# A two-direction scan block: where the absolute step sizes are read from, and where the fusion products stand in TensorE's order

## What is computed

```python
xz = x @ Win.T;  u, z = split(xz, 2)
uc = silu(convb + sum_k shift(u, k) * convw[:, k])      # 4 taps along the sequence
x_dbl = uc @ Wx.T                                       # 16 columns for dt, 32 for B, 32 for C
dt = softplus(x_dbl[..., :16] @ Wdt.T + bdt)
h_t = exp(dt_t * A) * h_(t-1) + dt_t * u_t * B_t        # the scan along the sequence
y = (h . C + uc * Dp) * silu(z)
out = layernorm(y @ Wout.T)
```

## Time and profile before

| | |
|---|---|
| median of 3 runs | 4335.14 us (4325.14 to 4340.07) |
| the profiled execution | 4339.85 us |
| its span, first to last instruction | 4338.3 us |
| mean granted clock of PE | 0.905 |
| scan stage | about the first 2,500 us |
| busy over the span: PE / DVE / ACT / POOL | 92% / 84% / 66% / 54% |

### The profile page before, as it was taken

One profiled execution on the slowest core, in us unless ns is written; L12 is line 12 of the kernel. 1 busy time (PEld: TensorE's weight loads), 2 busy tenths in 40 slices (PEclk: granted clock), 3 DMA queues, 4 the chain that ended last, 5 costly groups with the idle time before them and its releaser, 6 DMA issues. The chain is left out here.

```text
span 4338.3 us, 69764 instructions
## 1 busy us (share of the span) xinstructions
PE 4001.3 (92%) x19212; PEld 2993.2 (69%) x19213; DVE 3654.2 (84%) x6958; ACT 2850.2 (66%) x4732; POOL 2333.2 (54%) x1949
## 2 busy tenths in 40 slices
PE   6999999999999999999999959999999699999998
PEld 4666566566666666665665647887888588888887
DVE  7999999999999999999999938887888666666665
ACT  5777777777777777777777746666666344454444
POOL 2454545445454544545454456666666545555555
PEclk8989989888998989899898879888888799999999
DMA  2122121222222222222222212222222255555555
GB/s 69 46 45 42 46 42 47 42 48 46 42 47 41 47 42 48 46 42 45 42 48 42 43 47 88 78 79 75 78 78 79 107 99 94 96 104 93 87 95 85
DMA packets 198461, 272.58 MB, mean 63 GB/s; under 512 B 23377, under 2 KB 143058, under 8 KB 198354
## 3 DMA queue, kind: packets, MB, share of 16 engines
q0 software_dynamic: 94432, 130.60, 17.3%
q1 hardware_dynamic: 100480, 138.48, 11.4%
q10 hardware_dynamic: 3442, 2.21, 0.2%
HBM read 121.07 MB, written 150.14 MB: 63 GB/s over the span
## 5 line engine op out<-in xcount | busy, mean ns | idle before, releaser
L609 PE MATMUL pj<-xt,win 128*128 128x512 f32 x3144 | 920.5, 452 | 13.2 <-DVE uc L794 10.3
L609 PEld LDWEIGHTS pj<-xt,win 128*128 128x128 f32 x3144 | 675.5, 217 | 200.4 <-issue 46.7
L1983 POOL DMA_INDIRECT out<-e_y,e_to x272 | 471.8, 1734 | 366.8 <-ACT e_y L2089 306.1
L301 POOL TENSOR_TENSOR r<-r,neg_half 128x4 f32<-128x4 f32 x64 | 91.0, 1422 | 844.2 <-ACT r L384 844.2
L794 DVE SCALAR_TENSOR_TENSOR uc<-pj,convw,uc 128x511 f32<-128x511 f32 (+2 forms) x780 | 516.8, 728 | 5.4 <-ACT uc L408 5.4
L657 PE MATMUL po<-yz,wout 128*128 128x512 f32 x1024 | 483.6, 628 | 28.1 <-ACT fb L487 28.1
L326 POOL TENSOR_TENSOR wk<-v,uc 128x512 f32<-128x512 f32 x260 | 333.0, 1281 | 246.4 <-DVE v L842 245.6
L2034 PE MATMUL e_p<-e_w,e_a 128*128 128x256 f32 x3264 | 415.9, 284 | 0.8 <-DVE e_a L2144 0.8
L657 PEld LDWEIGHTS po<-yz,wout 128*128 128x128 f32 x1024 | 198.6, 199 | 310.2 <-issue 308.3
L2034 PEld LDWEIGHTS e_p<-e_w,e_a 128*128 128x128 f32 x3264 | 393.4, 188 | 11.1 <-DVE e_a L2144 3.0
L2022 PE MATMUL e_p<-e_xt,e_w 128*128 128x512 f32 x1632 | 395.2, 397 | 4.2 <-DVE e_xt L2136 2.4
(11 more groups left out here) (244 smaller groups left out, 9125.4 us busy)
## 6 DMA issues: line engine op xcount, KB each, us to landing
e_x<-expert_in SPq DMA_DIRECT2D x138, 260.0 KB, 2.6
bb<-bc SPq DMA_DIRECT2D x65, 512.0 KB, 5.3
h_rows<-fb POOLq DMA_DIRECT2D x64, 512.0 KB, 6.3
h_rows<-h0c SPq DMA_DIRECT2D x32, 512.0 KB, 2.9
a_h<-h_rows SPq DMA_DIRECT2D x128, 128.0 KB
out<-a_bs SPq DMA_DIRECT2D x128, 128.0 KB
bc<-xd SPq DMA_DIRECT2D x65, 128.0 KB, 2.2
e_w1s<-in_moe_w POOLq DMA_DIRECT2D x9, 512.0 KB, 5.7
```

The costliest lines, as they stand in the source:

```text
L609: i = mm(pj[m][:], win[d][wp][:, k, c:c + P], xt[xp][:, k, :], start=(k == 0 and n == 0), stop=(k == KD - 1 and n == 2))
L1983: pool.indirect_dma_start(out=out, out_offset=bass.IndirectOffsetOnAxis(ap=to[n][:, j:j + 1].bitcast(U32), axis=0), in_=y[n][:, j, :], in_ ...
```

## The change

The first copy of the step sizes, v, is now made for all four tiles first. |v| is then computed from v in SBUF, by halves, in a function of its own (`softplus_abs`): two operations of 128x1024 without a bias instead of four of 128x512 with one. `vc_ok` now counts halves. PE waits for `v_ok` instead of `vc_ok` before it overwrites `pj`. On ACT, `xt_copy` stands between Abs and Exp of the first half. `project_copies` writes `fo` ahead of `sq`. On PE the fusion products of a slot leave the end of `front` and stand in the next `front`, behind its first two gate tiles; as they overwrite the banks `po`, they also wait for `sq_ok`. The last slot's fusion stands behind the loop.

```diff
--- before.py
+++ after.py
@@ -436,15 +436,19 @@
                         act.wait_ge(S["da_ok"], MD * (t - 1) + m + 1)
                     act.activation(v[:, m, :], pj[m][:], ACT.Identity, bias=bdt[d][:, m:m + 1]
                                    ).then_inc(S["v_ok"], 1)
+
+            def softplus_abs(t, halves=range(NP)):
+                for h in halves:
+                    mm = slice(2 * h, 2 * h + 2)
+                    act.wait_ge(S["v_ok"], MD * t + 2 * h + 2)
                     if not (isinstance(t, int) and t == 0):
-                        act.wait_ge(S["g_ok"], NP * (t - 1) + m // 2 + 1)
-                    act.activation(lg[:, m, :], pj[m][:], ACT.Abs, bias=bdt[d][:, m:m + 1]
-                                   ).then_inc(S["vc_ok"], 1)
+                        act.wait_ge(S["g_ok"], NP * (t - 1) + h + 1)
+                    act.activation(lg[:, mm, :], v[:, mm, :], ACT.Abs).then_inc(S["vc_ok"], 1)
 
             def softplus_exp(t, halves=range(NP)):
                 for h in halves:
                     mm = slice(2 * h, 2 * h + 2)
-                    act.wait_ge(S["vc_ok"], MD * t + 2 * h + 2)
+                    act.wait_ge(S["vc_ok"], NP * t + h + 1)
                     if not (isinstance(t, int) and t == 0):
                         act.wait_ge(S["h_ok"], MD * (t - 1) + 2 * h + 2)
                     act.activation(y[:, mm, :], lg[:, mm, :], ACT.Exp, scale=-1.0).then_inc(S["y_ok"], 1)
@@ -474,8 +478,8 @@
                     act.wait_ge(S["o_ps"], KD * t + k + 1)
                     if not (isinstance(t, int) and t == 0):
                         act.wait_ge(S["f_ps"], 2 * t)
+                    act.activation(fo[:, k, :], po[k][:], ACT.Copy).then_inc(S["fo_ok"], 1)
                     act.activation(sq[:, k, :], po[k][:], ACT.Square).then_inc(S["sq_ok"], 1)
-                    act.activation(fo[:, k, :], po[k][:], ACT.Copy).then_inc(S["fo_ok"], 1)
 
             def finish(t, d):
 
@@ -536,6 +540,7 @@
             scan_weights()
             act.wait_ge(S["win_ok"], DIRS)
             v_copy(0, 0, range(MD))
+            softplus_abs(0)
             softplus_exp(0)
             softplus_sum(0)
             softplus_log(0)
@@ -546,11 +551,12 @@
                     t = 2 * s + d
                     front(t + 1, 1 - d, s + 1 if d == 0 else None)
                     more_states(t, d)
-                    v_copy(t + 1, 1 - d, range(2))
-                    softplus_exp(t + 1, (0,))
+                    v_copy(t + 1, 1 - d, range(MD))
+                    softplus_abs(t + 1, (0,))
                     if d == 0:
                         xt_copy(s + 1)
-                    v_copy(t + 1, 1 - d, range(2, MD))
+                    softplus_exp(t + 1, (0,))
+                    softplus_abs(t + 1, (1,))
                     softplus_sum(t + 1, (0,))
                     softplus_exp(t + 1, (1,))
                     if not (first and d == 0):
@@ -589,7 +595,7 @@
                 pe.wait_ge(S["xn_ok"], TT * (s + 1))
                 for k in range(KD):
                     if not (isinstance(s, int) and s == 0):
-                        pe.wait_ge(S["vc_ok"], MD * (2 * s - 1) + k + 1)
+                        pe.wait_ge(S["v_ok"], MD * (2 * s - 1) + k + 1)
                     for j in range(TT):
                         i = nc.tensor.transpose(pj[k][:, j * P:(j + 1) * P], xn[:, j, k * P:(k + 1) * P], ident[:])
                     i.then_inc(S["xt_ps"], 1)
@@ -602,7 +608,7 @@
                         pe.wait_ge(S["a_ok"], MD * t + m + 1)
                         pe.wait_ge(S["cv"], PAD * MD * t + last_tap(m))
                     elif not (isinstance(t, int) and t == 0):
-                        pe.wait_ge(S["vc_ok"], MD * (t - 1) + m + 1)
+                        pe.wait_ge(S["v_ok"], MD * (t - 1) + m + 1)
                     c = half * DI + m * P
                     for k in range(KD):
                         for n, (wp, xp) in enumerate(PARTS):
@@ -671,6 +677,7 @@
 
             def fusion(t, d):
                 pe.wait_ge(S["fo_ok"], KD * (t + 1))
+                pe.wait_ge(S["sq_ok"], KD * (t + 1))
                 for h in range(2):
                     for jj in range(2):
                         j = 2 * h + jj
@@ -682,6 +689,8 @@
             def front(t, d, s_next, turn, back):
 
                 in_proj(t, d, 1, range(2))
+                if back > 1:
+                    fusion(t - 2, d)
                 x_dbl(t, d)
                 in_proj(t, d, 1, range(2, MD))
                 dt_proj(t, d)
@@ -700,7 +709,6 @@
                 state_sum(t)
                 if back > 0:
                     out_proj(t - 1, 1 - d)
-                    fusion(t - 1, 1 - d)
 
             turn_x(0)
             pe.wait_ge(S["win_ok"], 1)
@@ -718,6 +726,7 @@
             slots(0, True)
             with pe.Fori(1, NSEQ) as s:
                 slots(s, False)
+            fusion(2 * NSEQ - 1, 1)
             row_squares(2 * NSEQ - 1, True)
```

## The result

| | before | after |
|---|---|---|
| median | 4332.1 us (4 runs, 4325.1 to 4340.1) | 4263.5 us (4 runs, 4249.8 to 4272.4) |
| ratio of the runs | | 0.9834, interval 0.9815 to 0.9854 |
| the profiled execution | 4339.85 us | 4265.17 us |
| the last `finish` operation of the scan stage starts at | 2512.5 us | 2442.0 us |
| the span after that | 1825.8 us | 1821.7 us |

The change takes 1.7% off by the ratio of the runs: 69 us by the medians, 70.5 us within the scan stage of the two profiles. The forecast was 44 us, the best bound 66. The forecast's signs and places were right, and one term of its sum, the clock, was not.

A forecast was written before the change was run, and what follows sets the result against it. VectorE was taken to bound the scan stage, waiting only for the logarithm and xt. 1.77 + 0.30 - 0.68 = 1.39 us per pair, times 32, is 44 us: median 4291, range 4262 to 4330.

The forecast's parts named there:

- the best bound: The sum without any low clock stretch: 1.77 + 0.30 = 2.07 us per pair, 66 us saved, 4269.
- the clock: PE drops to 1.2 GHz at its even-slot wait for the conv: 4 pairs in 10, costing 0.68 us per pair.
- DVE's two stops: VectorE's scan-stage waits: 2.22 us per pair for the logarithm ahead of L834, 0.65 for xt ahead of L781.
- Nothing else holds DVE: Claim that in the scan stage VectorE waits only for the logarithm and for xt.
- The odd chain: Odd slot, out projection to logarithm: 1.45 us shorter by moving fusion, 0.40 by step sizes from SBUF; 1.85 together.
- the stop at L834: VectorE's wait for the logarithm, 2.22 us per pair before; 1.77 of it was to go.
- Rival C: On ACT the wide Abs is not cheaper; gain 1.05 us per pair, 34 us, time 4301; chance 0.10.
- The even slot: x_dbl comes 1.1 us late but covered; the wait at L781 falls, gaining 0.30 us per pair if the clock holds.
- The new stop: PE standing 2.2 us in even slots, waiting for the conv ahead of the gates, where fusion had filled the hole.
- xt's wait: VectorE's wait at L781, mean 0.65 us per pair, forecast to fall to 0.35.
- A: Clock falls in every even slot; gates and fusion lose 1.70 us; 4323, no change that can be told; chance 0.17.
- B: Even slot's low-clock stretch is two stretches long, costing 3.40 us at L781; 43 us slower, 4378; chance 0.10.

## Why the prediction was right or wrong

**The bound.** DVE's two stops were the whole account. They fell from 2.87 to 0.73 us per pair, 2.14, times 32 is 68 us, and the medians differ by 69. "Nothing else holds DVE" is more than the rows show: the long operation beside POOL, 2.2 us per pair, was already in the earlier trace rows (3.50 at 1043.53). The change left it as it was, so the sum did not suffer.

**The odd chain: right.** 1.46 against 1.45 for the move, 0.39 against 0.40 for the wide Abs, 1.80 against 1.77 for the stop at L834. Rival C, the wide Abs no cheaper, is out: it takes 1.04 to 1.09 us, and the operation behind the second one starts 0.95 later.

**The even slot: right but for one term.** The new stop is there (1.70 us on average, forecast 2.2), and xt's wait did fall to near 0.35 (0.31): the gain of 0.30 came, 0.34.

**The clock: the failing term.** The step "I take 4 pairs in 10, 0.68 per pair" charged the new stop with a low stretch of 1.70 us in 4 pairs of 10. In the changed kernel the clock fell at it in none of 30 pairs: 0.68 x 32 = 22 us too much. With 4291 - 22 = 4269 the sum meets its own best bound, 5.5 us over the median. Of these, 3.0 are the median of the kernel before (4332.1 in these runs, 4335.1 in the forecast), and 2.2 the two other terms over 32 pairs, 1.80 against 1.77 and 0.34 against 0.30.

The mechanism is real: with the fusion move alone it came in 13 of 30 pairs at 1.6 us each, with one conv operation more in every second pair, with two at 2.6 us of waiting per pair. What the step had wrong in part is the stop, 1.70 us on average and not 2.2. I took the out projection to end before the conv of the even slot by as much as in one pair of before, one where PE had itself waited 1.17 us for ACT ahead of it. In the changed kernel that wait is left in 5 of 25 pairs only (3.8 us in all); in the others PE comes late with the out projection, and the stop is 1.4 to 1.7 us. That is not the whole of it: the stops of 2.15 to 2.18 us, as long as reckoned, held the clock too. Why they held, where stops of 1.80 to 2.10 us of the fusion move alone did not, stays open.

The Trainium skill (TensorE: Matmul & The Clock Gate, Why this matters for your kernels) warns of idle gaps between bursts of products. The Trainium skill's warning is of longer gaps than any stop at these gates, so it gives nothing for a stop of 2.2 us; in these runs the clock fell behind stops of 1.80 us and more. By an estimate from the Trainium skill's formula for an ACTIVATE (ScalarE: Activation LUTs, What ACT_TABLE_LOAD costs) the wide Abs would have saved 0.28 us per half, 0.56 for the two; the chain of two halves gained 0.39, which is what the rows gave.

**Rivals A and B: not here, but near.** With one conv operation of 0.66 us more at the stop the clock fell in half of the even slots, half of A. With two the time was A's, no change (0.9993), and a stretch of B's kind came in one pair of four.

**The range.** The bounds of the sum, 4269 to 4323, miss the median by 5.5 us; with the runs' scatter added, 4262, they reach 1.5 us under it. They were laid around a sum with a cost in it that no pair of this kernel had.

## What to carry to other kernels

Follow DVE's (the bound engine's) stops, sum them per turn of the loop, and price an edit on other engines only by what of those stops goes; that held here to a few per cent. Where an edit opens a hole in PE's work, work out the hole's length from the turns as they will be after the edit, not from one that had another wait in it; one conv operation more at this hole, 0.66 us, cost about 40 us here, half of it by the clock. Look also for single operations that take far longer than others of their shape: that is time lost inside the busy share. Test parts alone, but do not add them up: the two edits on ACT, the wide Abs and fo first, each gained about 25 us and gained 25 together; the move alone gained 29, and all three 69.

## What the runs showed that I had not expected

PE's clock can take back what a shorter chain gives. With the wide Abs, with fo first and with both, the pair was 75.1 us each time; with both, the pair came 1.1 us earlier in the trace, the clock rose when it had risen before, and the products took 0.53 us more. And the move is worth more with the other two than without: 0.84 us per pair for those two and 0.89 for the move alone make 1.73, the whole change gives 2.19. That it does so because its pair leaves the length of 75.1 us and its new stop costs no clock is argued and not shown.
